# Two PSUM banks for the heads and two for the scores in a fused attention and expert layer on one Trainium2 core

## The reference

```
xn = layernorm(x)
Q, K, V = xn @ Wq.T + bq, ctx @ Wk.T + bk, ctx @ Wv.T + bv      # 16 heads of 32
attn = softmax(Q K^T / sqrt(32))                                 # per head
x1 = x + tanh(g0) * ((attn V) @ Wo.T + bo)
xt = layernorm(x1);  p = softmax(xt @ router_w + router_b)       # 4096 tokens, 8 experts
e = argmax(p);  y = max(p) * (xt @ expert_w[e] + expert_b[e])
out = x1 + tanh(g1) * y
```

## Time and profile before

| | before |
|---|---|
| median of 3 runs | 1152.27 us (1151.54 to 1153.15) |
| the profiled execution's own time | 1165.53 us |
| its span, first to last instruction | 1163.8 us |
| mean granted TensorE clock | 0.955 |
| TensorE busy | 1032.3 us (89%) |
| VectorE busy | 805.2 us (69%) |
| POOL busy | 670.6 us (58%) |
| ScalarE busy | 513.1 us (44%) |

### The profile page before, as it was taken

One profiled execution on the slowest core, in us unless ns is written; L12 is line 12 of the kernel. 1 busy time (PEld: TensorE's weight loads), 2 busy tenths in 40 slices (PEclk: granted clock), 3 DMA queues, 4 the chain that ended last, 5 costly groups with the idle time before them and its releaser, 6 DMA issues. The chain is left out here.

```text
span 1163.8 us, 19046 instructions
## 1 busy us (share of the span) xinstructions
PE 1032.3 (89%) x5464; PEld 659.0 (57%) x5464; DVE 805.2 (69%) x1748; ACT 513.1 (44%) x920; POOL 670.6 (58%) x446
## 2 busy tenths in 40 slices
...
GB/s 231 76 74 121 66 67 68 141 75 98 69 138 78 91 76 134 74 83 91 129 81 73 117 106 74 69 120 104 78 64 90 253 73 81 164 154 120 136 118 46
DMA packets 70884, 119.39 MB, mean 103 GB/s; under 512 B 17854, under 2 KB 18878, under 8 KB 70656
## 3 DMA queue, kind: packets, MB, share of 16 engines
...
...
...
## 5 line engine op out<-in xcount | busy, mean ns | idle before, releaser
L1101 POOL TENSOR_TENSOR psum_keys<-psum_keys,probs 128x1024 f32<-128x1024 f32 x128 | 303.8, 2386 | 120.7 <-ACT probs L691 120.5
L691 ACT ACTIVATE probs<-sc 128x512 f32<-128x512 f32 x512 | 279.4, 598 | 210.5 <-PE sc L499 168.9
L826 DVE TENSOR_REDUCE maxima<-jb 128x1 f32<-128x512 f32 x512 | 323.3, 682 | 69.6 <-PE jb L519 68.6
L1101 POOL TENSOR_TENSOR psum_keys<-probs 128x1024 f32<-128x1024 f32 x64 | 153.5, 2412 | 228.9 <-ACT probs L691 228.9
L519 PE MATMUL jb<-k_stack,q_stack 96*128 96x512 f32 x512 | 197.1, 440 | 26.6 <-DVE maxima L826 10.8
L499 PE MATMUL sc<-q_stack,k_stack 98*128 98x512 f32 x512 | 193.6, 428 | 9.9 <-DMA q_stack<-max_rows 7.9
L519 PEld LDWEIGHTS jb<-k_stack,q_stack 96*128 96x128 f32 x512 | 98.2, 199 | 103.5 <-issue 40.7
L509 PE MATMUL hb<-probs,values 128*32 128x512 f32 x1024 | 141.7, 631 | 16.2 <-DVE heads_raw L845 8.0
L499 PEld LDWEIGHTS sc<-q_stack,k_stack 98*128 98x128 f32 x512 | 95.7, 194 | 82.8 <-ACT probs L691 29.6
L667 PE MATMUL sc<-e_hi,heads_hi 128*128 x156 | 68.6, 440 | 1.4 <-POOL e_lo L1128 0.9
L861 DVE SCALAR_TENSOR_TENSOR k_lo<-jb,bias,k_hi 128x512 fp32r<-128x512 f32 x32 | 23.9, 748 | 64.0 <-ACT k_hi L710 64.0
...
## 6 DMA issues: line engine op xcount, KB each, us to landing
...
k_stack<-k_lo SPq DMA_DIRECT2D x128, 64.0 KB, 2.0
q_stack<-q_lo SPq DMA_DIRECT2D x128, 64.0 KB, 2.0
...
```

The lines of the kernel that those rows point to most:

```text
L691: nc.scalar.activation(probs[:, kt % 2, h, :], scs[(16 * g + n) % NSC][:], ACT.Exp, scale=SCALE)\
L826: nc.vector.tensor_reduce(maxima[g % 2][:, n:n + 1], jbs[j][:], AX.X, ALU.max).then_inc(s["mx_done"], 1)
L1101: nc.gpsimd.tensor_tensor(psum_keys[:, two, :], in0, probs[:, kt % 2, two, :], ALU.add)\
```

## The change

PSUM is dealt out anew: `NSC` goes from 3 to 2, and the heads get two banks (`NHB = 2`), `hbs[g % 2]`.

- VectorE's `NM` multiplies in place, in the heads bank. ScalarE's `NM` and VectorE's `NL` read it there. `heads_raw` is only a `done` buffer of the expert stage, and the wait of `NM` for the `NL` before is gone.
- P0 of group g waits for `NL` of group g-2 (`nm_done`), not for `NM` of g-1.
- `TO` alternates between the heads banks and waits for `LO` n-2, not n-1. The first two wait for the last two `NL`.
- `HI` n (n below 4) waits for n+1 of the last batch's four output projections, not for all four.
- With two score banks, `S` n waits for `E` n-2, and `Y` n for `FI` n-2.
- All the item lists are written anew. In the bodies P0 stands earlier, and OP, V and K quarters stand elsewhere between the scores; POOL's list is shifted by about one body, its own sequence is nearly the old one. In `LAST` and `CLOSING` the order differs more: VectorE's `NM`, `W` and `PA`, POOL's gathers before W4 and W5, SP's W5 behind the last DR load, and `TO` n+2 ahead of `Y` n.

```diff
--- before.py
+++ after.py
 ORDER = {  "PE":
-        "1P3 1SUM 2S0 2S1 3M0 2S2 3M1 2S3 3M2 2S4 2S5 2S6 3M3 2S7 3M4 3M5 3M6 2S8 ^T4 2S9 2P0 2S10 3M7 3M8 2P1 ^T5 3M9",
-        "2S11 2S12 3M10 3M11 2P2 2S13 3M12 ^T6 ^T7 3M13 3M14 2S14 3M15 ^0Q ^0Qb ^0Qc ^0Qd 3MT ~RT3 ^0K 2S15 ^0Kb ^0Kc 3S0",
-        "^0Kd 3S1 3S2 3S3 2SUM 2P3 3S4 3S5 3S6 ~RL1 3S7 3P0 3S8 3S9 ^0M0 ^0M1 ^0M2 3S10 ^0M3 3P1 ^0M4 ^0M5 ^0M6 3S11 ^0M7",
...
+        "3Q 3Qb 1S2 1S3 3Qc 1S4 ~RC0 2M2 1S5 3Qd 1S6 1S7 3K 3Kb 3Kc 3Kd 1S8 1P0 ~LI0 2M3 1S9 2M4 1S10 1S11 2M5 2M6 2M7",
...
+        "1P2 ~RT2 1P3 2S0 2S1 2S2 1SUM 3M0 2S3 3M1 2S4 2S5 3M2 3M3 2S6 2P0 3M4 2S7 ^T4 3M5 3M6 2P1 3M7 3M8 2S8 2S9 ^T5",
+        "3M9 2S10 3M10 2S11 3M11 2S12 2P2 ^T6 3M12 2S13 ^T7 3M13 2S14 3M14 3M15 ^0Q ^0Qb ^0Qc ^0Qd ^0K ~RT3 3MT ^0Kb 2S15",
+        "^0Kc 2P3 3S0 3S1 ^0Kd 3S2 2SUM 3S3 3S4 3S5 3S6 ~RL1 3S7 3P0 3S8 3S9 ^0M0 ^0M1 3S10 ^0M2 ^0M3 3P1 ^0M4 ^0M5 ^0M6",
 OPENING = {
-        "~RW2 ^DC0 ^DC1 LW1 ^DC2 ~RW3 LC ^DC3 ^DX0 LW0 ^DX1 ^DX2 ^DX3 LW2 LW3 ^0SK ^0SQ",
+        "^DC0 ^DC1 LW1 ^DC2 LC ^DC3 ^DX0 ^DX1 ^DX2 LW0 ~RW2 ^DX3 LW2 LW3 ~RW3 ^0SK ^0SQ ^1SQ",
...
-        "WT0 WT1 WT2 TH ^LX0 WT3 ^LX1 ^LX2 ^LX3 ^T4 ^0K ^T5 WT4 ^T6 WT5 WT6 ^T7 WT7 WT8 ^0Q WT9 WT10 WT11 ^0M0 ^0M1 ^0M2",
...
+        "^LX0 WT0 ^LX1 WT1 WT2 WT3 ^T4 ^LX2 ^LX3 WT4 ^0K ^T5 ^T6 WT5 ^T7 WT6 TH WT7 WT8 ^0Q ^0M0 ^0M1 WT9 ^0M2 WT10 ^0M3",
 LAST = {  "DVE":
-        "3M10 3M11 3M12 3M13 3M14 3M15 ^T6 ^0M0 3MT ^0M1 ^0M2 ^0M3 ^0M4 ^0M5 ^1Q ^0M6 ^0M7 ~LR3 ^0M8 2SC ^0M9 ^0M10 W0",
-        "^0M11 2NM ~RS1 ~RC1 ^0M12 ^0M13 ~LI1 ^0M14 ~RG1 ^0M15 ^1M0 ^1M1 2NL ^1M2 ^1M3 ^1M4 ^1M5 W1 PA 3SC 3NM ^1M6 W6",
-        "^1M7 PC ^1M8 ^0MT ^1M9 ^1M10 ^2Q 3NL ^1M11 ^1M12 W2 ^1K OP0 LR0 OP1 LR1 ^1M13 ^T7 ^1M14 ^1M15 ^2K",
...
+        "3M5 ^T7 3M6 3M7 3M8 3M9 3M10 3M11 3M12 3M13 3M14 3M15 1NL ^0M0 ~LR3 ^0M1 ^LX2 ^0M2 3MT ^0M3 ^0M4 ^0M5 ^0M6 ^0M7",
+        "W0 ^0M8 ^2K ^0M9 2SC ^0M10 ^0M11 ~RS1 ^0M12 2NM ~RC1 ~RG1 ^0M13 ^0M14 ~LI1 ^0M15 2NL W1 ^1M0 ^1M1 PA ^1M2 ^1M3",
+        "W6 PC ^0MT ^1M4 3SC ^1M5 ^1M6 3NM 3NL ^1M7 ^1M8 W2 ^1M9 ^1M10 ^1M11 OP0 LR0 ^1M12 ^1M13 ^1M14 OP1 LR1 ^1M15 ^LX3",
 CLOSING = {
     "SP": [
-        "W0 ~DR1 ~DR2 W1 W6 W2 W3 W4 W5 ~~RW2 ~DR3 ~~RW3 W7 EB ~RW0 ~RW1 ~RW2 ~RW3",
+        "W0 ~DR1 ~DR2 W1 W6 W2 W3 W4 ~~RW2 ~~RW3 ~DR3 W5 W7 EB ~RW0 ~RW1 ~RW2 ~RW3",
     ],
-        "~OP0 ~OPb0 ~OPc0 ~OPd0 ~OP1 ~RT0 ~OPb1 ~OPc1 ~OPd1 ~OP2 ~OPb2 ~OPc2 ~OPd2 TO0 ~RT1 ~OP3 ~RT2 ~OPb3 ~OPc3 ~OPd3",
-        "~RL0 TO1 Y0 TO2 ~RC0 Y1 TO3 ~RT3 Y2 TO4 Y3 TO5 ~RL1 TO6 Y4 TO7 Y5 TO8 Y6 ~LI0 TO9 Y7 ~RC1 TO10 Y8 TO11 Y9 ~LI1",
...
+        "~OP0 ~OPb0 ~OPc0 ~OPd0 ~OP1 ~OPb1 ~OPc1 ~OPd1 ~RT0 ~OP2 ~OPb2 ~OPc2 ~OPd2 ~OP3 TO0 ~OPb3 ~RT1 TO1 ~OPc3 ~RT2",
+        "~OPd3 TO2 TO3 ~RT3 ~RL0 Y0 TO4 Y1 ~RC0 Y2 Y3 TO5 TO6 Y4 TO7 ~RL1 ~LI0 Y5 ~RC1 TO8 Y6 TO9 Y7 Y8 TO10 Y9 TO11 TO12",
...
-        "~2A4 ~2A5 ~OP0 ~~LR1 ~3A0 ~3A1 ~3A2 ~3A3 ~3A4 ~3A5 ~OP1 ~OP2 GA0 GA1 ~OP3 W4 GA2 ~LR0 W5 GA3 GA4 GA5 GA6 SE0 GA7",
...
+        "~OP0 ~2A4 ~2A5 ~~LR1 ~3A0 ~3A1 ~3A2 ~3A3 ~3A4 ~3A5 ~OP1 GA0 ~OP2 GA1 GA2 GA3 GA4 W4 ~OP3 ~LR0 W5 SE0 GA5 GA6 GA7",
...
-NJB, NSC = 4, 3
+NJB, NSC, NHB = 4, 2, 2
...
         scs = [ps(f"sc{i}", [P, S]) for i in range(NSC)]
-        hb = ps("hb", [P, S])
+        hbs = [ps(f"hb{i}", [P, S]) for i in range(NHB)]
...
                     if n == 0:
-                        wait(pe, s["nm_chain"], g)
+                        wait(pe, s["nm_done"], g + 1 - NHB)
...
                         last = nc.tensor.matmul(
-                            hb[h * HD:(h + 1) * HD, :], values[:, n, (HG * c + h) * HD:(HG * c + h + 1) * HD],
+                            hbs[g % NHB][h * HD:(h + 1) * HD, :], values[:, n, (HG * c + h) * HD:(HG * c + h + 1) * HD],
                             probs[:, n % 2, h, :], start=(n == 0), stop=(n == NT - 1))
                     last.then_inc(s["pv_done"], 1)
...
                 elif kind == "TO":
-                    if n == 0:
-                        wait(pe, s["nm_chain"], NG * B)
+                    if n < NHB:
+                        wait(pe, s["nm_done"], NG * B + n + 1 - NHB)
                     pe.wait_ge(s["xe"], n + 1)
-                    wait(pe, s["lo"], n)
+                    wait(pe, s["lo"], n + 1 - NHB)
...
-                        last = nc.tensor.transpose(hb[:, k * P:(k + 1) * P], xe[n % 2][:, k * P:(k + 1) * P], ident[:])
+                        last = nc.tensor.transpose(hbs[n % NHB][:, k * P:(k + 1) * P], xe[n % 2][:, k * P:(k + 1) * P], ident[:])
...
-                    nc.scalar.activation(heads_hi[:, c, :], heads_raw[:], ACT.Identity,
+                    nc.scalar.activation(heads_hi[:, c, :], hbs[g % NHB][:], ACT.Identity,
                                          bias=bias[:, 2, c:c + 1]).then_inc(s["nm_hi"], 1)
...
                 elif kind == "HI":
                     act.wait_ge(s["tp"], n + 1)
-                    wait(act, s["op_mm"], NT * B)
+                    wait(act, s["op_mm"], NT * (B - 1) + min(n + 1, NT))
...
-                    nc.scalar.activation(xt_hi[n % WORK], hb[:, :].rearrange("p (k q) -> p k q", q=P), ACT.Copy)\
+                    nc.scalar.activation(xt_hi[n % WORK], hbs[n % NHB][:, :].rearrange("p (k q) -> p k q", q=P), ACT.Copy)\
...
-                    wait(dve, s["nm_done"], g)
-                    nc.vector.tensor_tensor(heads_raw[:], hb[:], sums[:], ALU.mult).then_inc(s["nm_chain"], 1)
+                    nc.vector.tensor_tensor(hbs[g % NHB][:], hbs[g % NHB][:], sums[:], ALU.mult).then_inc(s["nm_chain"], 1)
...
-                    nc.vector.scalar_tensor_tensor(heads_lo[:, c, :], heads_raw[:], bias[:, 2, c:c + 1],
+                    nc.vector.scalar_tensor_tensor(heads_lo[:, c, :], hbs[g % NHB][:], bias[:, 2, c:c + 1],
                                                    heads_hi[:, c, :].bitcast(F32), ALU.add, ALU.subtract)\
...
                 elif kind == "LO":
                     dve.wait_ge(s["hi"], n + 1)
-                    nc.vector.tensor_tensor(xt_lo[n % WORK], hb[:, :].rearrange("p (k q) -> p k q", q=P),
+                    nc.vector.tensor_tensor(xt_lo[n % WORK], hbs[n % NHB][:, :].rearrange("p (k q) -> p k q", q=P),
                                             xt_hi[n % WORK].bitcast(F32), ALU.subtract).then_inc(s["lo"], 1)
```

More of the change, by code:

```diff
@@ L34 @@
     "SP": [
-        "~~RW2 ~~RW3 1SQ ^DC0 1SK 2SQ 2SK ^DC1 ~RW0 ^DC2 ^DC3 ~RW1 ~DR2 ~DR3 3SQ ^DX0 ^DX1 ^DX2 3SK ^DX3 DR0 DR1 ^0SQ",
-        "^0SK",
+        "~~RW3 1SK 2SQ 2SK ^DC0 ^DC1 ~RW0 ~RW1 ^DC2 ^DC3 ~DR2 ~DR3 3SQ ^DX0 ^DX1 3SK ^DX2 ^DX3 DR0 DR1 ^0SQ ^0SK ~RW2",
+        "^1SQ",
     ],
     "PE": [
[10 rows of a table removed]
[10 rows of a table added]
     ],
     "ACT": [
[5 rows of a table removed]
[5 rows of a table added]
     ],
     "DVE": [
[5 rows of a table removed]
[5 rows of a table added]
     ],
     "POOL": [
-        "C3 ~1A3 ~~OP2 ~~OP3 ~1A4 ~1A5 LX0 ~2A0 LX1 ~2A1 LX2 LX3 ~2A2 ~OP0 ~2A3 ~2A4 ~2A5 ~~LR1 ~3A0 ~3A1 ~3A2 ~3A3 ~3A4",
-        "~3A5 ~OP1 0A0 0A1 0A2 0A3 0A4 0A5 ~LR0 1A0 1A1 ^C0 ^C1 ^C2 1A2",
+        "~~2A4 ~~2A5 ~~3A0 ~~3A1 ~~3A2 ~~3A3 ~~3A4 ~~3A5 ~0A0 ~~OP0 ~0A1 ~~OP1 ~0A2 ~0A3 ~0A4 ~0A5 ~~LR0 ~1A0 ~1A1 C0 C1",
+        "C2 ~1A2 C3 ~~OP2 ~1A3 ~~OP3 ~1A4 ~1A5 LX0 LX1 ~2A0 ~2A1 LX2 LX3 ~2A2 ~~LR1 ~2A3",
     ],
```

16 lines of the change are left out of this document (6 added, 10 removed), and 113 rows, old and new, of tables (CLOSING, LAST, OPENING, ORDER).

## The result

The changed kernel is slower. Its four runs have a median of 1178.32 us (1169.35 to 1182.78) beside 1152.71 for the kernel before; the ratio is 1.0184, 95% interval 1.0143 to 1.0225. Timed again in a later round (`after_again`) it was 1184.63 beside 1156.39, ratio 1.0225 (1.0179 to 1.0271). The forecast was 1135, range 1118 to 1156.

What follows compares the result with a forecast made beforehand. Steady bodies were taken as bound by TensorE, with losses in the last body, the boundary and the expert stage. Terms 15-3-13-14-2 = -17 us took 1152.3 to 1135 us, range 1118 to 1156.

Steps and rivals of the forecast that it cites:

- The expert stage: Expert tiles: a second heads bank spares transposes the wait for LO, winning half of 27 us lost; -14 us.
- Rival B: Expert stage waits for gathers and ScalarE, so two heads banks give only 4 us; 1145 us, chance 0.18.
- Two score banks: Attention bodies: scores wait longer for exponentials, partly swallowed by existing idle time; +15 us, bounds 7 and 35.
- The walk over the new list: Stall count along TensorE's new list with two score banks: eight short places a body, 22.5 us more in all.
- Rival A: Bodies: ScalarE's queue makes two score banks too few, 40 us in place of 15; 1160 us, chance 0.19.
- P0 without NM: Start of each group's P: no more waiting for VectorE's multiplication NM; -3 us (0 to -4).
- Operands in PSUM: NL and ScalarE's NM reading heads from PSUM: 32 NL save 8 us of VectorE's time, most in the last body.
- Last body and boundary: Last body up to Y0: removes part of 13.6 us of TensorE waits; -13 us, bounds -4 and -18.
- Y0 near 984: Sign in the profile that the forecast is right: first Y near 984 us; later than 992 would mean rival C.
- The opening: Start of the kernel: VectorE's first statistics and the transposes of x come first; -2 us (0 to -4).

Runs made afterwards that it cites:

- the short exponential: Exponential over only 64 of 512 columns from the ninth score tile on; ratio 0.9982 in the kernel before (control), 1.0092 in the changed kernel.
- before_two_waits: The kernel before with S n waiting for E n-2 in place of n-3 and four P items moved ahead; 1222.26 us, ratio 1.0563.
- banks_alone2: The changed kernel's new banks and waits with the lists of before, except four P items moved ahead; 1229.76 us, ratio 1.0614.

## Why the prediction was wrong, point by point

**The expert stage** (forecast -14, bounds -5 and -22; measured +8 and +15) is the step that turned the sign. Two sentences failed. "Y waiting for FI n-2 in place of n-3 costs nothing as long as FI comes within 3.23 us of its Y": the condition does not hold. FI is up to 9.5 us late, and the wait alone cost 17.5 us with the lists of before; with the new lists it shows as 3 to 6 us of waits, and the rest of the loss, in late rows and in the rebuilt lists, stays open. The trace of the kernel before had the lateness already: in it FI n began more than 3.23 us after the end of Y n for 16 of the 39 tiles, up to 7.4 us. And "of the 27 us lost I take half": the second bank alone gave nothing (0.9999, interval 0.9964 to 1.0033). I had seen that the rows came late behind the longest waits, and still counted the waits by the releaser that they named. Rival B had that half right (4 us) and not the other.

**Two score banks** (+15, bounds 7 and 35; first S of batch 0 to batch 7: +20 to +29, with -3 for P0 in it). The walk over the new list, 22.5 us in all, was nearer than the +15 that I took: the extra stalls were not swallowed by those already there. A steady body was forecast at 112 to 115 and took 115.3. But the walk explains it only in part, since about a third goes with the length of E, and for the old lists it gave 4 to 5 us where 8 were measured. Rival A asked for 4 us per body and for the gains; it had the sign, but not the reason for all of it: a body cost 3.3 us, which by its own rule (4 us) was not yet slower, and its time, 1160, was 18 us short of the 1178 measured, since it kept the gain in the expert stage.

**P0 without NM** (-3): the waits on NM are gone (8.0 us), those of P on exponentials grew by 7.5 us. By the sums nothing was won; that these are the same waits moved is argued, not shown, and with the short exponential P waited for it only 4.6 us.

**Operands in PSUM.** NL at a median of 742 ns, against 743 with the SBUF operand and 747 for Q's low part, as forecast. The table of the Trainium skill, page VectorE: DVE Perf Modes, section on the TRN2 errata, gives more fixed cost to a source in PSUM, by which I had estimated an NL 65 ns longer; the trace doesn't show it (1 ns shorter). I had put 8 us of VectorE's time and none of TensorE's. Measured: without it the changed kernel is 10 us longer. The long NL came with two SBUF operands in both lists (longest 7.22 and 2.71 us), and never with one in PSUM (longest 0.75). The Trainium skill, page SBUF — State Buffer, section Who interferes with whom, has a VectorE instruction with two SBUF inputs contend with a POOL instruction that reads SBUF, and one with a single SBUF input not; the rows agree, a median of 1658 ns against 742.

**Last body and boundary** (-13 up to the first Y, bounds -4 and -18): measured 140.8 against 148.9 us, -8.1, within the bounds. Up to SA it was -12.6, of which some is moved behind it, since `3SC 3NM`, which followed PA, now stand behind W6 and PC as well; the boundary gave 4.5 back, to VectorE's W7 and, 2.2 us ahead of it, POOL's second split. Of the causes that I named two gave little when tried alone: W0 moved gave nothing, and heads in SBUF cost 1.1 to 2.0 us there. For the second heads bank the record has a hint only: with the lists of before and two score banks the stretch took 135.0 us in `before_two_waits`, where P0 waited 4.7 us for NM, and 128.5 in `banks_alone2`, which has the new heads banks and no such wait (different chips, one trace each). What in the new lists shortens the stretch was not isolated. POOL, called nearly full there, had room: it was busy 25.5 of the 33 us from 936 to 969.

**Y0 near 984** was not what my own sum gave. It took the -13 off 997.5 and left out +15, -3 and -2, which all fall ahead of Y0: 994.5. Measured were 998.85 and 1007.77, so Y0 could not serve as a sign for the last body.

**The opening** (-2): first S at 57.0 and 57.8 us against 60.0 and, in the first trace of before, 59.6: -2 to -3. Over all traces it is less: seven with the new opening list have a mean of 57.6 (55.2 to 59.5), nine with the old one 58.9 (58.0 to 60.0). Right, within its bounds.
